# Issuing every attention-score matmul twice in an adaLN, Mamba and attention kernel

## The reference, cut to what matters

```
q = (xn @ q_w + q_b).reshape(B, L, H, hd)
k = (xn @ k_w + k_b).reshape(B, L, H, hd)
v = (xn @ v_w + v_b).reshape(B, L, H, hd)
scores = jnp.einsum('bqhd,bkhd->bhqk', q, k) * hd ** (-0.5)
scores = jnp.where(causal[None, None], scores, -jnp.inf)
attn = jax.nn.softmax(scores, axis=-1)
attn_out = jnp.einsum('bhqk,bkhd->bqhd', attn, v).reshape(B, L, Dm) @ o_w + o_b
...
h = jnp.exp(dtt[..., None] * A) * h + (xt * dtt)[..., None] * Bt[:, None, :]
y = jnp.einsum('bn,bdn->bd', Ct, h)
```

## Time and profile before

| what | value |
|---|---|
| time, median of 3 runs | 2040.51 us (2033.99 to 2044.25) |
| profiled execution, its own time | 2044.78 us |
| its span, first to last instruction | 2043.1 us |
| mean granted TensorE clock | 0.782 |
| PE busy | 1742.4 us (85%) |
| DVE busy | 1394.9 us (68%) |
| ACT busy | 1079.6 us (53%) |
| POOL busy | 841.3 us (41%) |

### The profile page before, as it was taken

The page is one execution under the profiler, slowest core; times in us unless marked ns, Lnnn a source line. Parts: engine busy times, 40 slices in busy tenths (PEclk is TensorE's granted clock), DMA queues, the critical chain, the costliest instruction groups (busy, mean ns, idle before and its releaser), DMA issues. The chain is left out here.

```text
span 2043.1 us, 21887 instructions
## 1 busy us (share of the span) xinstructions
PE 1742.4 (85%) x7090; PEld 952.8 (47%) x7090; DVE 1394.9 (68%) x2071; ACT 1079.6 (53%) x1784; POOL 841.3 (41%) x863
## 2 busy tenths in 40 slices
PE   4958979979878879888799887887999999989878
PEld 3334423333333333333333333645877877763673
DVE  1596766767767767767667833858776868766876
ACT  3734444444454454454444436646778787852107
POOL 1363545535535444455455523112122222226762
PEclk8865676676776776767766768988999999985879
DMA  2111101101111111111011002110111111100001
GB/s 74 68 57 58 53 23 61 52 31 54 46 53 42 49 59 36 36 63 50 24 61 52 22 1 62 31 49 14 52 47 38 46 42 47 42 21 0 1 1 41
DMA packets 61678, 84.74 MB, mean 41 GB/s; under 512 B 6600, under 2 KB 32062, under 8 KB 61566
## 3 DMA queue, kind: packets, MB, share of 16 engines
q1 hardware_dynamic: 61466, 83.31, 13.1%
q10 hardware_dynamic: 100, 0.03, 0.0%
HBM read 74.38 MB, written 8.78 MB: 41 GB/s over the span
## 5 line engine op out<-in xcount | busy, mean ns | idle before, releaser
L993 PE MATMUL bank<-QK 48*128 48x128 bf16 (+7 forms) x1024 | 303.9, 381 | 110.7 <-DVE Mx L1242 67.7
L1682 POOL TENSOR_TENSOR dBx<-dtx,Bb 128x512 f32<-128x512 f32 x256 | 321.4, 1277 | 16.1 <-DMA Bb<-b_dram 9.6
L1553 ACT ACTIVATE bank<-dtv,alog 128x512 f32<-128x512 f32 x256 | 176.3, 690 | 263.1 <-DVE hst L1262 262.3
L1242 DVE TENSOR_REDUCE Mx<-bank 128x1 f32<-128x384 f32 (+3 forms) x352 | 220.2, 632 | 137.2 <-PE bank L993 135.0
L1295 DVE TENSOR_TENSOR hl<-lsq,hh 128x512 fp32r<-128x512 f32 x320 | 257.0, 814 | 81.8 <-ACT hh L1569 73.5
L1662 POOL TENSOR_SCALAR_AFFINE_SELECT PT<-PT 128x256 f32<-128x256 f32 (+1 forms) x320 | 118.0, 372 | 465.7 <-ACT PT L1509 465.4
L1262 DVE TENSOR_TENSOR_SCAN hst<-bank,dBx 128x512 f32<-128x512 f32 x256 | 297.9, 1204 | 4.5 <-POOL dBx L1682 4.5
L1509 ACT ACTIVATE PT<-bank 128x512 f32<-128x512 f32 x320 | 185.0, 591 | 208.4 <-PE bank L993 206.7
L1566 ACT ACTIVATE lsq<-bank,vcol 128x512 f32<-128x512 f32 x320 | 218.7, 692 | 112.8 <-DVE hl L1295 69.4
L1180 DVE SCALAR_TENSOR_TENSOR yT<-bank,bc,yT 128x256 f32<-128x256 f32 x480 | 203.8, 478 | 90.5 <-PE bank L1096 90.5
L993 PEld LDWEIGHTS bank<-QK 48*128 48x128 bf16 (+1 forms) x1024 | 72.1, 100 | 355.0 <-issue 161.7
(11 more groups left out here) (247 smaller groups left out, 2531.3 us busy)
## 6 DMA issues: line engine op xcount, KB each, us to landing
Bb<-b_dram SPq DMA_DIRECT2D x128, 256.0 KB, 3.4
stage<-w_rows SPq DMA_DIRECT2D x64, 256.0 KB, 3.2
parts<-part SPq DMA_DIRECT2D x16, 384.0 KB, 2.8
QK<-parts SPq DMA_DIRECT2D x64, 96.0 KB
QK<-parts SPq DMA_DIRECT2D x64, 64.0 KB
stage<-in_L_ffn_We_dram SPq DMA_DIRECT2D x16, 256.0 KB, 3.2
hst<-in_L_attn_x_dram SPq DMA_DIRECT2D x8, 256.0 KB, 5.5
QK<-parts SPq DMA_DIRECT2D x64, 32.0 KB
```

The source lines that it names most:

```text
L993: return engine.matmul(o, l, r, start=start, stop=stop, tile_position=pos, skip_group_check=True)
L1242: engine.tensor_reduce(Mx[:, it["u"] % 2, qi, h:h + n], o[:, 0:P * (qi + 1) * n].rearrange("p (i c) -> p i c", i=n), AX.X, ALU.max).then_i ...
L1553: engine.activation(bank[4 + h][:], dtv[:, b % 2, h, :], ACT.Exp, scale=alog[:, h, n:n + 1]).then_inc(sems["act_da"], 1)
L1682: engine.tensor_tensor(dBx[:, sl, h], dtx[:, b % 2, h], Bb[:, sl], ALU.mult).then_inc(sems["pool_dbx"], 1)
```

## The change

Each matmul of a "max" and of an "att" step is issued again into the same columns of the same bank, before the mask matmul or the signal to ACT. In "att" the second pass starts its accumulation afresh, so it writes the same values. In "max" with several heads in one bank the order is all heads, then all heads again; head 0 of each pass starts the accumulation and the others no longer do, where before each head did.

```
                     q.wait_ge(it["ready"], ("pool_set", pool_set["idb"]), it["free"])
-                    for i in range(n):
+                    for i in (*range(n), *range(n)):
                         a = it["a"] + i
                         mm(o[:, kc * i:kc * i + kc], QK[64 * h:64 * h + 48, 0, s, a, P * qi:P * qi + P], QK[64 * h:64 * h + 48, 1, s, a, 0:kc],
-                           stop=False)
+                           start=(i == 0), stop=False)
...
                     q.wait_ge(it["ready"], ("ld_one", 32), it["free"])
-                    for i, kj, off in it["parts"]:
+                    for i, kj, off in (*it["parts"], *it["parts"]):
```

## The result

The changed kernel takes 2177.32 us (median of 4 runs, 2175.98 to 2186.43) against 2039.82 us: 137 us more, ratio 1.069, 95% interval 1.066 to 1.072. The forecast was 2231 in a range of 2135 to 2300, slower at 0.93. The direction and the range held, and the size was given 40% too large: +191 for +137.

What follows compares the result with a forecast made beforehand. PE was taken to bound the mixer stage in its stretches at 0.50 (1.2 GHz). 16.3 + 4.5 = 20.8 us a batch, 23.9 with the clock falling, gave +191 us over eight batches: 2231 us, range 2135 to 2300.

Steps and rivals of the forecast that it cites:

- the step that was called the most likely to fail: Mixer stage: the granted clock; a mean above 0.75 would put the time under 2165, below 0.60 above 2280.
- Which stage, and what bounds it: Only the mixer stage is at stake, PE sets the pace at 0.50 (1.2 GHz); the last 783 us stay.
- The price of one: Score matmuls: a repeat costs only its columns, 0.267 us at 0.50 and 0.133 at 1.00 for 320 columns.
- The rival of bare weight loads: Repeats' weight loads in the mixers hide nowhere: 98 us on top of 191, 2330 us; chance 0.06.
- The 0.11 us that were put down to other weights and rows: Score matmuls: time beyond the columns, paid once where the next operation has other weights and rows.
- Where they land: Per mixer batch, 61 repeats at 0.50 cost 16.3 us and 67 at 1.00 cost 8.9 us.
- What hides: Mixer stretches at 1.00: half of the 8.9 us a batch, 4.4, falls into PE's waits; nothing hides at 0.50.
- The clock: Mixer batches: s falls a little, 0.45 to 0.38, taking the added cost from 20.8 to 23.9 us a batch.
- s: Share of a mixer batch's work at the upper clock level, 0.45 before, forecast 0.38.
- The formula of that step: With the change, a mixer batch takes 186 - 49 s us; 167.4 us at s of 0.38.
- The rival that ends on the other side: Mixer clock rises nearly always and pays for the work: faster from s = 0.87, 1988 us at s = 1; chance 0.04.

Runs made afterwards that it cites:

- the short repeats: Ahead of each score matmul the same one with 32 columns, against the kernel before: 2061.98 us, ratio 1.013.
- the control on 48 rows: Instead of repeats, filler matmuls (`identb` by `mask`, same column counts) on 48 rows ahead of each step's score matmuls, against the kernel before: 2173.79 us, ratio 1.064.
- five times: Every score matmul issued five times, against once in the kernel before: 2633.78 us.
- One kind alone: Only the "max" or only the "att" matmuls issued twice, against the kernel before: 2144.02 us (ratio 1.050) and 2126.66 us (ratio 1.043).
- three times: Every score matmul issued three times, against once in the kernel before: 2238.23 us.
- "max" alone: Only "max" matmuls issued twice, against before: 2144.02 us; in the section on other kernels, the 128-row filler in "max" steps only: ratio 1.0005.
- the filler on 128 rows: Instead of repeats, `identb` by `mask` with the same column counts on 128 rows ahead of both kinds of step, against before: 2011.53 us, ratio 0.987.
- the short filler: One filler matmul of 128 rows and 128 columns ahead of each "max" and "att" step, against the kernel before: 2065.33 us, ratio 1.010.
- "att" alone: The filler matmuls on 128 rows in the "att" steps only, against the kernel before: 2004.38 us, ratio 0.980.

## Why the prediction was right, and where it was off

The stage, the engine that sets the pace and the direction were right. The size was 40% too large, and the time stands inside the range because that was wide enough for the clock, the step that was called the most likely to fail.

**Which stage, and what bounds it.** Right: the tail kept its length, the whole loss lies in the mixers, PE stayed the bound at 0.50 and ACT, DVE and the transposes waited longer for it.

**The price of one.** Right: 0.42 us for 512 columns at 0.50 and 0.22 at 1.00 where 0.43 and 0.21 were forecast. The rival of bare weight loads (2330 us) is out; the short repeats price 1024 loads at nothing that can be told from zero. The 0.11 us that were put down to other weights and rows go with the rows: in the control on 48 rows, filler and score matmul of 512 columns have different weights and take the same 0.96 us together at 0.50 (680.12 to 681.08).

**Where they land.** The sum was right within 1 us a batch: 24.6 us of added score work against 16.3 + 8.9 = 25.2. The two terms were not: the views give 18.0 at 0.50 and 6.6 at 1.00. That these misses of about 2 us cancel is luck.

**What hides.** Right: 5.0 us a batch of idle time used up against 4.4.

**The clock.** This step failed. I wrote that s, the share of the work at the upper level, falls from 0.45 to 0.38, and charged 3.1 us a batch for it. By the same reckoning it stayed: 48.25 / 0.61 = 79.1 of 79.1 + 95.26, 0.45. For the rest of PE's work alone it rose: 25.7 / 0.61 of 100.0 us is 0.42, 26.7 / 0.61 of 98.1 is 0.45, and this work became 2.5 us cheaper. So in place of 3.1 us of cost stand 2.5 of gain. These 5.6 of the 7 us between 23.9 and 16.9 a batch come from here, and the remaining ones from the two small differences above. The formula of that step was too dear besides: with the true s it gives 186 - 49 x 0.45 = 164 for 160.4 us measured.

The reason that I gave for it, that score matmuls of 48 rows in a full queue do not lift the clock, is borne out: 71.6 us without a gap at 1.2 GHz in five times, and 162 us between fillers that differ in their rows. What was wrong was to go from there to a clock that falls evenly with the dose; the 41.0 us at 2.4 GHz in five times show that the same work need not end the upper level. One kind alone lowers it to 0.65, both leave it at 0.68, three times raise it to 0.72, five times give 0.68 again. A reading that fits, and that no run shows, is that the repeats do two things, crowd the queue at 0.50 and fill gaps at 1.00, and that which of them wins changes with the dose and with where the work stands in time. The traces do show that a kernel settles into a cycle: from one Mamba output projection (`zg,wso`) to the next, batch after batch takes 143.4 us before, 160.4 after the change, 157.0 with "max" alone and 218.5 at five times, each within 0.1 us once it has settled and until the last batch; at three times it goes back and forth between 170.0 and 174.8. So a cost here is the difference between two such cycles, counted eight times, and need not add up from its parts. Why it goes up at three and down at five is not settled: I have no run that holds the order in time fixed while the dose changes.

**The rival that ends on the other side** needed s of 0.87. None of the amounts of repeats that were run came near; the filler on 128 rows did get the time below before's. That rival named a mechanism that exists for a different instruction: TensorE work that uses all rows can pay for itself here, as it did in "att" and in both, and did not in "max" or as the short filler. The advice of the Trainium skill, TensorE: Matmul & The Clock Gate, on why this matters for kernels, to keep the engine continuously busy, is not enough here: with the filler PE is busy 88% of the mixer stage on 128 rows and 89% on 48, at a clock of 0.84 and of 0.68.

## What to carry to other kernels

In a stage that PE bounds and whose granted clock is well below 1.00, price an added or removed matmul twice: by its columns, and by what it does to the clock of everything around it; here the same 164,000 columns on 48 rows moved the rest of PE's work by +26, +16 or -19 us, depending on where they stood. Ask how many rows it uses: small contractions (heads of few channels) take columns like any other and did not lift the clock. Where such work sets the pace, a cheap matmul on 128 rows beside it is worth a run, in each kind of step by itself: here "att" alone gave 39 us, both gave 27, "max" alone nothing, and a shorter one cost 21.

## What the runs showed of the hardware that was not expected

- Two fillers with equal columns and places, on 128 and on 48 rows, give a mixer stage of 1153 us at a clock of 0.84 and of 1320 us at 0.68.
- A gap-free 71.6 us of PE, two thirds of it matmuls of 48 or 49 rows, is granted 1.2 GHz from end to end, and the 41.0 us behind it with the same share of such matmuls 2.4 GHz; with the filler on 128 rows 78.5 us with 8 us of gaps are granted 2.4 GHz.
- 1024 further weight loads of the same weights, each behind a matmul of only 32 columns, cost together no more than 23 us, columns included.
- The second pass over all score matmuls costs 137 us, the third 61, the fourth and fifth together 396: neither constant nor growing evenly.
